# Attention on the whole TensorE array in three bf16 parts, instead of two row tiles in two F32R parts

## What is computed

```
q = x @ W_q                                   # 16 heads of 16 columns
latent = (x @ W_k + x @ W_v) @ W_down_kv      # 64 columns
k_rec, v_rec = latent @ W_up_k, latent @ W_up_v
scores = einsum('bhqd,bhkd->bhqk', q, k_rec) / sqrt(256)
scores = scores * exp(-0.01 * |tq - tk|)      # decay over positions
out = softmax(scores) @ v_rec                 # 16 batch entries x 16 heads, 1024 x 1024 scores each
out @ W_o
```

## Time and profile before

| | us |
|---|---|
| median of 3 runs | 6592.82 |
| lowest, highest | 6590.03, 6598.11 |
| the profiled execution | 6590.99 |
| its span, first to last instruction | 6589.2 |

### The profile page before, as it was taken

How to read it: one execution, slowest core, us unless ns; L and a number is a source line. 1 busy time by engine, 2 the same in 40 slices (tenths; PEclk the granted TensorE clock), 3 DMA queues, 4 the chain that set the end, 5 groups by cost and what they waited for, 6 DMA issues and landing times.

```text
span 6589.2 us, 111578 instructions
## 1 busy us (share of the span) xinstructions
PE 5587.2 (85%) x37644; PEld 3442.7 (52%) x37644; DVE 4583.0 (70%) x10398; ACT 3414.6 (52%) x4949; POOL 2681.9 (41%) x2116
## 2 busy tenths in 40 slices
PE   5579994799898999998999998999999975499992
PEld 5468883344444444444444444444444445488871
DVE  7645553577877877877777778778777847555674
ACT  1134442366666666666666666656666631144430
POOL 6710003444435445444444454344443127500266
PEclk9999997588999999999999999989999965599996
DMA  5433333555555555555555555556555425333486
GB/s 173 164 98 105 105 104 95 105 106 111 104 114 109 104 117 105 107 120 97 113 111 105 108 114 103 112 102 114 114 90 96 73 81 179 132 105 104 141 262 215
DMA packets 497050, 777.19 MB, mean 118 GB/s; under 512 B 77299, under 2 KB 373365, under 8 KB 471925
## 3 DMA queue, kind: packets, MB, share of 16 engines
q1 hardware_dynamic: 447348, 635.77, 43.4%
q0 software_dynamic: 49152, 134.28, 6.6%
HBM read 442.35 MB, written 327.42 MB: 117 GB/s over the span
## 4 chain that ended last, share of the span: by engine, by line
PE 59%; DVE 23%; POOL 9%; issue 6%; ACT 1%; DMA 1%; SPq 0%; POOLq 0%; DVEq 0%; ACTq 0%
PE psum L1069 13%; PE psum L346 11%; DVE at_mx L1198 10%; PE psum L938 9%; POOL xs L617 7%; PE psum L959 7%; PE psum L363 5%; DVE at_Sd L1194 4%; DVE at_mab L1203 3%; PE psum L947 3%; PE psum L1009 2%; PE psum L335 2%; PE psum L354 2%; PE psum L1044 2%; DVE at_mp L1217 1%
## 5 line engine op out<-in xcount | busy, mean ns | idle before, releaser
L1198 DVE TENSOR_REDUCE at_mx<-psum 128x4 f32<-128x512 f32 x3584 | 2222.9, 681 | 737.7 <-PE psum L938 735.7
L1140 ACT ACTIVATE at_P<-psum 128x1024 f32<-128x1024 f32 x2048 | 2074.8, 1023 | 863.4 <-PE psum L947 832.0
L938 PE MATMUL psum<-at_kst,at_qst 48*128 48x128 f32 (+3 forms) x7168 | 1867.2, 373 | 238.6 <-DVE at_mx L1198 187.2
L938 PEld LDWEIGHTS psum<-at_kst,at_qst 48*128 48x128 f32 x7168 | 1084.9, 194 | 1124.3 <-DVE at_mx L1198 799.9
L959 PE MATMUL psum<-at_qst,at_kst 50*128 50x512 f32 (+3 forms) x5120 | 1557.1, 393 | 0.0
L1069 PE MATMUL psum<-at_P,at_V 128*17 128x512 f32 x8192 | 1169.6, 645 | 0.0
L947 PE MATMUL psum<-at_ident,at_Sd 64*128 64x64 f32 x4096 | 924.9, 263 | 42.9 <-ACT at_P L1140 12.6
L959 PEld LDWEIGHTS psum<-at_qst,at_kst 50*128 50x128 f32 x5120 | 860.1, 208 | 0.0
L1285 POOL TENSOR_TENSOR at_Sd<-at_Sd,at_m 128x1024 f32<-128x1024 f32 x256 | 483.8, 1903 | 674.9 <-DVE at_m L1213 673.0
L947 PEld LDWEIGHTS psum<-at_ident,at_Sd 64*128 64x128 f32 x4096 | 510.9, 140 | 426.1 <-PE psum L959 361.7
L1237 POOL DMA_INDIRECT at_xT<-ys,at_yib x256 | 245.8, 960 | 788.2 <-DMA at_gab<-table 711.2
(11 more groups left out here) (245 smaller groups left out, 7798.0 us busy)
## 6 DMA issues: line engine op xcount, KB each, us to landing
parts<-at_hl SPq DMA_DIRECT2D x256, 512.0 KB, 4.4
at_kst<-parts SPq DMA_DIRECT2D x768, 128.0 KB
at_qst<-parts SPq DMA_DIRECT2D x768, 128.0 KB
m2X<-xs SPq DMA_DIRECT2D x272, 128.0 KB, 2.0
ys<-m2X SPq DMA_DIRECT2D x272, 128.0 KB, 1.7
m1X<-xs SPq DMA_DIRECT2D x264, 128.0 KB, 2.0
ys<-m1X SPq DMA_DIRECT2D x264, 128.0 KB, 1.7
m2X<-x SPq DMA_DIRECT2D x64, 512.0 KB, 4.3
```

The lines of the kernel that those rows point to most:

```text
L938: ins = e.matmul(to[:, col - 512 * u:col - 512 * u + ln], self.qst[r:r + 48, s, side, 128 * t:128 * t + 128], self.kst[r:r + 48, s, 1 - si ...
L1140: e.activation(self.P[:, i % NP, :], slot[a % 2], ACT.Exp).then_inc(self.taken.sem, 1)
L1198: e.tensor_reduce(self.mx[:, p % 2, hh, 8 * o + 4 * u:8 * o + 4 * u + 4], of, op=ALU.max, axis=AX.X).then_inc(self.s_read.sem, 1)
```

## The change

The parts become bf16: three parts (hi, middle, low) of each number and a stack of 96 rows, six products of parts, plus 3 rows for the maximum. Each head has its own stack from partition 0, so it takes the whole array's rows. `scores` of one head, then `turned` of the other, are issued one after the other, not alternately; Sd's diagonal block is transposed in one instruction of 128 rows. The number of columns is what it was.

What follows from it: a projection takes one more ScalarE copy and one more GpSimd subtraction (`part` 0 and 1), and the first ScalarE copy moves into the same segment as `scale`; `send` issues six DMAs for two; `stack` issues 18 DMAs of 64 KB for 12 of 128 KB. `mlo` becomes three VectorE instructions, each waiting for the one before, and it and `msend` move from right behind `mturn` to the head of the next step's items. `fold` is split: one head after the step of the diagonal, the other a step later. The statistics of the norm take four segments for two, so what follows them moves two steps later. `norm` starts one step later than before.

```diff
-        self.qst, self.kst = sb("qst", [128, NS, 2, S], F32R), sb("kst", [128, NS, 2, S], F32R)
+        self.qst, self.kst = sb("qst", [99, 2 * NS, 2, S], BF16), sb("kst", [99, 2 * NS, 2, S], BF16)
...
+            if split is not None:
+                yield from (("mlo", split), ("msend", split))
+                split = None
             if score or turn:
                 yield ("step", score, turn)
+            if fold is not None:
+                yield ("fold", fold, 1)
+                fold = None
             if score and score[1] == self.DIAG:
-                yield ("fold", score[0])
+                yield ("fold", score[0], 0)
+                fold = score[0]
...
             if after and after[0][0] <= s:
-                p_max = after.pop(0)[1]
-                yield from (("mturn", p_max), ("mlo", p_max), ("sub", 2 * p_max), ("msend", p_max))
+                split = after.pop(0)[1]
+                yield from (("mturn", split), ("sub", 2 * split))
...
             yield ("stats", b, t)
-            if t == 3:
+            if t % 2 and t < 7:
                 yield None
...
-            yield from (("project", b, i), None, ("scale", b, i), None, ("hi", b, i), ("lo", b, i), None, ("send", b, i))
+            yield from (("project", b, i), None, ("scale", b, i), ("part", b, i, 0), None, ("part", b, i, 1), None, ("send", b, i))
...
-        yield from (("norm", p), None, ("share", p))
+        yield from (None, ("norm", p), None, ("share", p))
...
+                    for c, (r0, r1) in enumerate(((0, 3), (3, 5), (5, 6))):
+                        for r in range(r0, r1):
+                            e.dma_start(qd[16 * r:16 * r + 16], src[0, h, c]).then_inc(done, 16)
+                    e.dma_start(kd[0:48], src[1, h].rearrange("c d v t -> (c d) v t")).then_inc(done, 16)
+                    e.dma_start(kd[48:80], src[1, h, 0:2].rearrange("c d v t -> (c d) v t")).then_inc(done, 16)
+                    e.dma_start(kd[80:96], src[1, h, 0]).then_inc(done, 16)
...
+                for col, t, key, ln, side in self.score_pieces(o):
+                    if col // 512 == u:
+                        ins = e.matmul(bank[(z + u) % 3][:, col - 512 * u:col - 512 * u + ln], self.qst[0:96, s, side, 128 * t:128 * t + 128],
+                                       self.kst[0:96, s, 1 - side, key:key + ln], start=True, stop=True)
+                ins.then_inc(self.s_filled.sem, 1)
...
+            for qh in range(2):
+                for q0, ln, side in self.turned_pieces(kb, qh):
+                    e.matmul(slot[a % 2][:, q0:q0 + ln], self.kst[0:99, s, side, 128 * kb:128 * kb + 128],
+                             self.qst[0:99, s, 1 - side, q0:q0 + ln], start=True, stop=True)
             w.wait_ge(*self.shifted.at(2 * p + 2 - hh))
+            e.transpose(slot[a % 2][:, 128 * kb:128 * kb + 128], self.Sd[:, (2 * p + hh) % 4, kb, :], self.ident[:]).then_inc(self.filled.sem, 1)
...
                 for hh in range(2):
-                    work = ([scores(2 * score[0] + hh, score[1], z + 2 * hh)] if score else []) + ([turned(*turn, 1 - hh)] if turn else [])
-                    if turn and hh:
-                        rest(*turn, 1)
-                    while work:
-                        work = [g for g in work if next(g, 1) != 1]
+                    if score:
+                        scores(2 * score[0] + hh, score[1], z + 2 * hh)
+                    if turn:
+                        turned(*turn, 1 - hh)
...
-                e.tensor_tensor(self.mp[:, p % 2, 1, :], self.mT[:, p % 2, :], self.mp[:, p % 2, 0, :].bitcast(F32), ALU.subtract).then_inc(self.m_parts.sem, 1)
+                k = own.end(e.tensor_tensor(mT, mT, mp[:, 0], ALU.subtract))
+                w.wait_ge(*k)
+                k = own.end(e.tensor_copy(mp[:, 1], mT))
+                w.wait_ge(*k)
+                e.tensor_tensor(mp[:, 2], mT, mp[:, 1], ALU.subtract).then_inc(self.m_parts.sem, 1)
...
+                w.wait_ge(*self.part_hi.at(2 * j + c + 1))
+                e.tensor_tensor(pt[:, j % 2, 2] if c else qs[:], qs[:], pt[:, j % 2, c], ALU.subtract).then_inc(self.part_lo.sem, 1)
```

More of the change, by code:

```diff
@@ L661, in __init__ @@
         self.qr, self.qs = sb("qr", [128, 512]), sb("qs", [128, 2, 512])
[L662 removed]
+        self.pt = sb("pt", [128, 2, 3, 2, 512], BF16)
         self.OT, self.OF = sb("OT", [128, 8, D]), sb("OF", [128, 2, 512])
@@ L688, in __init__ @@
         self.y_in, self.x1_out = sig.new("a_y_in", 256 * B), sig.new("a_x1_out", 16 * B)
-        self.m_out, self.parts_out = sig.new("a_m_out", 16 * NPAIR), sig.ring("a_parts_out", [32 * 4 * B] * 2)
-        self.stacked = sig.ring("a_stacked", [192 * n for n in shares_of(NPAIR, NS)])
+        self.m_out, self.parts_out = sig.new("a_m_out", 16 * NPAIR), sig.ring("a_parts_out", [96 * 4 * B] * 2)
+        self.stacked = sig.ring("a_stacked", [288 * n for n in shares_of(NPAIR, NS)])
         self.m_rows = sig.ring("a_m_rows", [64 * n for n in shares_of(NPAIR, NS)])
@@ L711, in order @@
         ahead = [i for b in range(1, B) for i in ((b, self.gather_order(b)), (b, self.prep_order(b)))]
-        late, after = [], []
+        late, after, split, fold = [], [], None, None
         def advance(queue):
@@ L930, in scores @@
         def scores(n, o, z):
-            s, r = n // 2 % NS, 64 * (n % 2)
-            w.wait_ge(*self.stacked[s].at(192 * (n // 2 // NS + 1)))
+            s = n % (2 * NS)
+            w.wait_ge(*self.stacked[n // 2 % NS].at(288 * (n // 2 // NS + 1)))
             for u in range(2):
-                to = bank[(z + u) % 3]
                 w.wait_ge(*self.s_read.at(z + u - 2))
-                runs = [run for run in self.score_pieces(o) if run[0] // 512 == u]
-                for col, t, key, ln, side in runs:
-                    ins = e.matmul(to[:, col - 512 * u:col - 512 * u + ln], self.qst[r:r + 48, s, side, 128 * t:128 * t + 128],
-                                   self.kst[r:r + 48, s, 1 - side, key:key + ln], start=True, stop=True)
-                    if col == runs[-1][0]:
-                        ins.then_inc(self.s_filled.sem, 1)
-                    yield
@@ L953, in turned @@
             w.wait_ge(*self.shifted.at(2 * p + 2 - hh))
-            diagonal(p, kb, hh, r)
-            yield
-            for qh in (d, 1 - d):
-                runs = self.turned_pieces(kb, qh)
-                for q0, ln, side in runs:
-                    ins = e.matmul(slot[a % 2][:, q0:q0 + ln], self.kst[r:r + 50, s, side, 128 * kb:128 * kb + 128],
-                                   self.qst[r:r + 50, s, 1 - side, q0:q0 + ln], start=True, stop=True)
-                    if qh == d and q0 == runs[-1][0]:
-                        ins.then_inc(self.near.sem, 1)
-                    yield
@@ L965, in rest @@
-        def rest(p, kb, hh):
-            w.wait_ge(*self.near.at(16 * p + 2 * kb + 2 - hh))
-            diagonal(p, kb, hh, 64 - 64 * hh).then_inc(self.filled.sem, 1)
+            e.transpose(slot[a % 2][:, 128 * kb:128 * kb + 128], self.Sd[:, (2 * p + hh) % 4, kb, :], self.ident[:]).then_inc(self.filled.sem, 1)
         z = 0
@@ L1199, in vector @@
             if kind == "fold":
-                p = at[0]
-                w.wait_ge(*self.s_read.at(z))
-                for hh in range(2):
-                    last_fold = own.end(e.tensor_reduce(self.mab[:, 1, 8 * hh:8 * hh + 8], self.Sd[:, (2 * p + hh) % 4], op=ALU.max, axis=AX.X))
+                p, hh = at
+                w.wait_ge(*self.s_read.at(32 * p + 4 * self.ORDER.index(self.DIAG) + 4))
+                last_fold = own.end(e.tensor_reduce(self.mab[:, 1, 8 * hh:8 * hh + 8], self.Sd[:, (2 * p + hh) % 4], op=ALU.max, axis=AX.X))
             if kind == "max":
```

69 lines of the change are left out of this document (30 added, 39 removed).

## The result

The kernel after takes 6745.44 us in the median of 4 runs (6737.1 to 6749.83) against 6591.42 for the kernel before, run beside it: ratio 1.0241, 95% interval 1.0209 to 1.0272. The forecast was slower with 0.75, and 6820; it is slower, by 154 us where 229 were forecast, and 5 us above the lower end of the likeliest case's range (6740 to 6920). Later runs of both kernels, side by side on one chip, gave 6759.6 against 6600.2, ratio 1.0244 (1.0196 to 1.0293).

The account below looks back on a forecast made before the run. The prediction took the loop through the ring of three banks, not one engine, as the bound. It summed 6591 + 20 + 204 + 98 - 65 - 30 = 6818, taken as 6820; range 6540 to 7030 us, likeliest 6740 to 6920.

Parts of the forecast that it names:

- likeliest case: The forecast's main case: the kernel after slower, at 6740 to 6920 us, chance 0.50.
- TensorE's columns and the ring: Attention step: a half 0.93 to 0.98 us without row tiles; columns and three-bank ring both give about 3.02 a step.
- tiles were worth more: Rival: the ring hides nothing, every step grows by 0.28 us more than counted, +287, 7100 us; chance 0.11.
- shorter step: Rival: serial order fills the banks in time, steps of 2.75 us, -276, so 6540 us; chance 0.20.
- The bare pair: Pair with only gathering beside it: 27.0 us against 26.8, or +20 us for 128 pairs.
- mlo against GpSimd: Three chained VectorE instructions of mlo each wait for one whole GpSimd instruction: +204 us, bounds 0 and +280.
- half the lock: Rival: VectorE gets in after one GpSimd instruction or the copy is free; 6640 to 6720 us, chance 0.14.
- ScalarE held by part: ScalarE waits at the part copy behind GpSimd with exponentials queued, in two pairs an entry: +98 us, bounds 0 and double.
- several hundred us: Sign of the forecast: ScalarE's total wait for GpSimd at the part copy.
- What goes away: Newton step leaves the two sub, -65 us; hidden waits for mlo, -30; clock gains and losses set against each other.
- the terms 20 - 77 - 65 - 30: Bare pair +20, its 0.6 a pair for mlo taken out, Newton step -65, hidden waits for mlo -30 us.
- DMA: Stack and send transfers: same stack bytes, more issues, longer steps leave time; free, within the 1.5 us left.

Follow-up runs that it names:

- the last pairs of the comparison above: Pairs 6 and 7 at full clock: kernel before with folds, statistics, norm changed and mlo on GpSimd, 25.7 and 25.6 us; whole array medians 25.7 and 25.1.
- the maximum in two parts: Kernel after with the negated maximum in two bf16 parts instead of three, mlo one VectorE instruction: 0.943 of before, attention stretch 3966 us.
- scale early: Kernel after with scale in the segment of project, ahead of the sub that waits for the maximum: 0.975 of before, attention stretch 4200 us.
- both repairs: Kernel after with mlo on GpSimd and scale in the segment of project: 6306.6 us, 0.956 of before, attention stretch 3786 us.
- the list's changes: Kernel before, F32R and row tiles kept, with folds over two steps, statistics in four segments, norm one step later: 0.952 of before, attention stretch 4064 us.
- the first and third group: Two of three groups of follow-up runs, each on one chip; the kernel before took 7149 and 7184 us there.

## Why the forecast was right, and where its sizes were off

**TensorE's columns and the ring: right.** 0.93 to 0.98 for a half, measured 0.94; 2.93 to 3.02 for a step, measured 2.98; a bf16 matmul of 512 columns starts 0.22 to 0.23 us before the next, the pace of the F32R one in rows 5. The rival "tiles were worth more" falls with the last pairs of the comparison above, and the rival "shorter step" with the 2.98. The rule of the Trainium skill, TensorEngine Tiling (Array Packing), Overview, holds for the half (0.59 against 0.94, 1.6 times where the page has up to two) and not for the step; that VectorE's reads of the ring already held it is argued, as said above.

**The bare pair: right.** 27.0 forecast with GpSimd idle, 26.5 measured: 4.50 for the turn of the maximum (4.6), 7.17 for the diagonal and the next (7.3), 2.96 to 2.99 for a plain step (3.02). The difference to before has the other sign, -0.4 for +0.2 (which is 26 us for 128 pairs, not the 20 of the sum), both at full clock.

**mlo against GpSimd: right.** The term (+204, and 0.6 a pair within the bare pair's sum, 281 together) measured 254 by the run with the maximum in two parts and 242 by that with `mlo` on GpSimd; up to 124 and 88 of that is the clock, which the prediction did not count here. TensorE's wait for VectorE's reads, 351 us against 73, is the direct sign. The copy to bf16 waits like the others (1.80 beside a multiply of 1.94, 0.21 alone), so the rival "half the lock" falls too; the Trainium skill's exclusive lock of the shared port pair (SBUF — State Buffer, on the two separate sides) is what the trace shows for this form as well.

**ScalarE held by part: too small.** The step "6.5 x 15 = +98" measures 192 once `mlo` no longer takes its turn at the same place, and 20 while it does. The place was right (pairs 3 and 4: 7.0 and 2.6 us); the late exponentials, the late turn of the maximum behind them and a clock that fell were not counted. The 192 is one way to share out what the two hold together: taken in the other order, scale early gives 20 and `mlo` 414. Only the sum, 434 us, does not depend on the order, and the terms for both (204 + 77 + 98) make 379. The sign "several hundred us" of ScalarE waiting at the copy came out at 195.

**What goes away: far too small.** The prediction had -65 for the Newton step and -30 for hidden waits, and set the clock against itself. With both repairs the change is 290 us faster than the kernel before (3786 against 4076), where the terms 20 - 77 - 65 - 30 make -152. This is the part of the sum that was off, and it is why 6820 was 75 us too high: the two costs were 55 more than forecast and the gains 138 more, together 83 less; the other 8 us are that the traced run of the kernel after is that much faster than its median. So the closeness of 6820 is in part luck: each side was counted too small, and they cancel.

What the 290 consist of is not settled. Up to 207 of it is time at the lower clock (254 against 47), the effect that the prediction set to nothing. The bare pair shows a part without the clock: pair 6 is 25.7 with both repairs and 26.9 before at full clock; 1.2 us for all 128 pairs would be 154, where the terms 20 - 77 have -57. But the kernel with row tiles, the list's changes and `mlo` on GpSimd has the same 25.7, so the bf16 stacks have no part in that. The repair itself takes from VectorE also the one `mlo` instruction that the kernel before has there; in the kernel after one such instruction cost about nothing (3966 with it, in the run with two parts, 3978 without), and in the kernel with tiles no run separates it from the list. The list's changes by themselves show 4064 against 4076 in the kernel before, on another chip and at a lower clock. Put back one at a time, the statistics' segments cost 195 to 289 and the folds with norm 160, where 65 and some 80 were counted; these do not add up to the gain, since the first moves the whole preparation and the Newton step is only 3.3 us an entry of it. The -30 was not tested.

**DMA: nothing, right.** TensorE waits once, 18 us, for the transfers of the stacks between 1200 and 5000 us, where it waited 20 before, and not for the maximum's rows. The sizes were wrong: `stack` issues 12 DMAs of 64 KB and two each of 192, 128 and 64 KB, not 18 of 64; the sum is that of 12 of 128, as said.

What is still open is how the clock shares in each of these: it moved with every stall (0.86 to 0.99 in the stretch), the bounds above only say at most how much, and no run holds it fixed.

## What to carry to other kernels

Splitting one short VectorE instruction with two SBUF operands into a chain of three costs not three times its length but up to one whole GpSimd instruction for each; look at what GpSimd has queued at that moment, or put the chain on GpSimd, where it took 1.1 us and waited for nothing in between. Before a tile layout is kept for its speed on TensorE, see in the step's chain whether TensorE's columns are what the step waits for, and compare stretches at the same clock. And where two engines hold the same pair in turn, test the two repairs together: here one gave 242 us, the other 20, both 434, so neither has a share of its own.

## What the runs showed of the hardware that was not expected

The same kernel takes 6600 or 7150 to 7184 us, by the chip. The F32R kernel before has a mean granted TensorE clock of 0.90 to 0.92 on one and 0.84 to 0.86 on the others, while the bf16 kernels have 0.89 to 0.94 over all three. Each chip was used at one time only, so chip and time are not told apart. On the chips of the first and third group the order of the two kernels may well turn round: the variant with scale early, whose attention is 20 to 38 us shorter than that of the kernel after, is 2.5% faster than the kernel before on the chip of the first. An estimate for the kernel after there, its stretch of 4220 between the 1310 us ahead and the 1473 behind of that variant, is 7000 against 7149. The kernel after itself was not run on these chips.

The transfers of the stacks, the same bytes in rows of 4 KB for 8 KB, took less of the DMA engines: the busy share of all transfers in attention went from 0.55 to 0.33. In the traces a packet of 8192 bytes took 0.95 us in the mean in the kernel before, one of 4096 bytes 0.24 us in the kernel after; what else than the size did it is not separated.
